# A fused attention and gated-recurrence kernel: ScalarE's zT copies put first, the head's loads in one queue, and six tiles of the output added by DMAs

## The reference

```python
x = x + layernorm(attention(layernorm(x)))
x = x + layernorm(gated(layernorm(x)))
```

```python
q = (x @ Wq.T).reshape(N, S, H, hd).transpose(0, 2, 1, 3)     # same for k, v
att = softmax(einsum('nqhd,nkhd->nhqk', q, k) / sqrt(hd), axis=3)
out = einsum('nhqk,nkhd->nqhd', att, v).reshape(N, S, D) @ Wo.T + bo
```

```python
ft = sigmoid(xt @ wf.T + c @ uf.T + bf); it = sigmoid(xt @ wi.T + c @ ui.T + bi)
gt = tanh(xt @ wc.T + c @ uc.T + bc);    c = ft * c + it * gt
h = tanh(einsum('tbi,oi->tbo', x, wo) + c_final @ uo.T + bo)
```

## Time and profile before

| what | us |
|---|---|
| median of 3 runs | 1361.56 |
| lowest and highest | 1359.27 and 1363.56 |
| the profiled execution, its own time | 1356.45 |
| its span, slowest core (core 6) | 1354.9 |
| spans of the 8 cores | 1345.2 to 1354.9 |
| mean granted TensorE clock of the cores | 0.989 to 0.993 |

### The profile page before, as it was taken

How to read it: one execution, slowest core, us unless ns; L and a number is a source line. 1 busy time by engine, 2 the same in 40 slices (tenths; PEclk the granted TensorE clock), 3 DMA queues, 4 the chain that set the end, 5 groups by cost and what they waited for, 6 DMA issues and landing times.

```text
span 1354.9 us, 25960 instructions; the slowest of 8 cores (1345.2 to 1354.9 us)
## 1 busy us (share of the span) xinstructions
PE 1296.4 (96%) x8256; PEld 733.4 (54%) x8256; DVE 834.1 (62%) x1460; ACT 571.9 (42%) x1572; POOL 400.9 (30%) x879
## 2 busy tenths in 40 slices
PE   4989999999899999899999999999999999999995
PEld 2577777776677777454444444444444444444442
DVE  5357778988799976574554545545455453226887
ACT  1246666665566665563222222222222222212665
POOL 3014444555455543331110101101011010001876
PEclk9999999999999999999999999999999999999998
DMA  9985676899789867728331222312222112009878
GB/s 198 197 143 115 147 152 143 190 188 184 187 196 197 203 195 266 265 71 277 128 125 47 94 91 80 125 48 94 92 80 94 48 63 78 0 15 346 272 253 248
DMA packets 126085, 200.96 MB, mean 148 GB/s; under 512 B 72672, under 2 KB 78816, under 8 KB 122848
## 3 DMA queue, kind: packets, MB, share of 16 engines
q1 hardware_dynamic: 109536, 172.56, 40.5%
q0 software_dynamic: 16416, 26.74, 14.6%
HBM read 157.34 MB, written 83.89 MB: 178 GB/s over the span
## 4 chain that ended last, share of the span: by engine, by line
PE 82%; DMA 5%; DVE 3%; SPq 3%; issue 2%; ACT 2%; POOL 2%; DVEq 0%; POOLq 0%; ACTq 0%
PE ps_big L445 11%; PE ps_s L445 11%; PE ps_s L433 11%; PE ps_big L433 11%; PE ps_big L320 11%; PE ps_big L346 7%; PE ps_big L308 6%; PE ps_big L329 3%; PE ps_s L504 3%; PE ps_big L504 2%; PE ps_o L504 2%; DMA exr<-xr 2%; PE ps_o L382 2%; SPq L1145 1%; PE ps_s L365 1%
## 5 line engine op out<-in xcount | busy, mean ns | idle before, releaser
L991 POOL TENSOR_SCALAR pn<-p,rl 128x128 bf16<-128x128 f32 x512 | 180.5, 368 | 298.2 <-DVE rl L601 297.6
L876 ACT ACTIVATE p<-ps_s,nm 128x128 f32<-128x128 f32 x512 | 181.0, 366 | 115.1 <-DVE nm L605 106.8
L346 PE MATMUL ps_big<-wo,zT 128*128 128x512 bf16 x512 | 122.9, 384 | 13.5 <-ACT zT L887 10.2
L691 DVE SCALAR_TENSOR_TENSOR ti<-ti,tg 128x512 f32<-128x512 f32 x64 | 44.2, 690 | 141.8 <-ACT tg L927 141.8
L308 PE MATMUL ps_big<-wv,xT 128*128 128x512 bf16 x512 | 123.1, 388 | 0.7 <-DVE zb L587 0.5
L320 PE MATMUL ps_big<-xT,wq 128*128 128x256 bf16 x1024 | 122.1, 274 | 0.0
L320 PE MATMUL ps_big<-xT,wk 128*128 128x256 bf16 x1024 | 121.2, 273 | 0.0
L605 DVE TENSOR_REDUCE nm<-ps_s 128x4 f32<-128x512 f32 x128 | 88.4, 691 | 29.0 <-PE ps_s L365 26.0
L876 ACT ACTIVATION_READ_ACCUMULATOR p<-ps_s,nm 128x1 f32 x512 | 104.2, 203 | 0.0
L320 PEld LDWEIGHTS ps_big<-xT,wq 128*128 128x128 bf16 x1024 | 98.2, 98 | 11.0
L320 PEld LDWEIGHTS ps_big<-xT,wk 128*128 128x128 bf16 x1024 | 97.7, 98 | 10.8
(11 more groups left out here) (162 smaller groups left out, 2479.1 us busy)
## 6 DMA issues: line engine op xcount, KB each, us to landing
z_scr<-zb SPq DMA_DIRECT2D x32, 512.0 KB, 6.2
h<-x_scr SPq DMA_DIRECT2D x29, 512.0 KB, 6.8
out<-h SPq DMA_DIRECT2D x28, 512.0 KB, 4.1
xin<-x SPq DMA_DIRECT2D x26, 512.0 KB, 6.6
zb<-z_scr SPq DMA_DIRECT2D x24, 512.0 KB, 4.2
xrb<-xr SPq DMA_DIRECT2D x24, 512.0 KB, 3.5
x_scr<-xrb SPq DMA_DIRECT2D x24, 512.0 KB, 2.9
vst<-v_scr SPq DMA_DIRECT2D x64, 128.0 KB, 6.6
```

What stands on the lines that cost most here:

```text
L346: mm = t.matmul(bank[:], zT[u % 2][:, ft * 128:(ft + 1) * 128], wo[:, ft * D + half * 512:ft * D + half * 512 + 512], start=ft == 0, stop= ...
L876: ex = a.activation(p32[G % 2][:, c], psS[G % 2][:, c], AF.Exp, bias=nm[G % 2][:, pk:pk + 1], accum_out=ls[G % 2][:, pk:pk + 1])
L991: op = g.tensor_scalar(pn[G % 2][:, c], p32[G % 2][:, c], rl[G % 2][:, pk:pk + 1], 1.0, AL.mult, AL.mult)
```

## The change

Four things change.

1. *The head's loads.* SP loads only tiles 0 and 1 of x, without a wait, and goes straight on to the masks. Tiles 2 to 7 are issued by POOL, behind V0; V1, K0, K1, Q0 and Q1 are issued one by one between the calls of rstd1, and wo last.
2. *The head's order.* DVE takes apply1(u) and stats1(u + 2) in turns. TensorE flips tiles 0 and 1 first, and tile i from 2 to 7 right ahead of group i. The copy of the flips 0 to 7 moves from DVE to ACT. In ACT's slots the copy of zT (oevict) now stands first, in all odd slots from 5 to 127; the even slots from 112 lose it, but for 128 and 130.
3. *Two buffers.* xl[4] and xl[5] move from the xln buffers to the region of exr. ACT's evict of F(., 1) no longer waits for flip2(5); in its place DVE's cell(0, 4) does, and SP waits for p_ap and d_ex1 instead of s_t1.
4. *The output.* ACC are now tiles 24 to 29 (before 24, 26, 27), VectorE's are 3, 7, 11, 15, 19, 23, 30, 31 (before ... 28, 29, 31). With it the residual of 25, 28 and 29 goes into the output directly, and their loads and stores fall away.

```diff
-H_DVE = (3, 7, 11, 15, 19, 23, 28, 29, 31)
-H_ACC = (24, 26, 27)
+H_DVE = (3, 7, 11, 15, 19, 23, 30, 31)
+H_ACC = (24, 25, 26, 27, 28, 29)
...
-          + [xln[0], xln[1], vtok[0], vtok[1]])
+          + [at(f"xl{i}", [128, D], BF16, oXR + o) for i, o in ((4, 6144), (5, 4096))]
+          + [vtok[0], vtok[1]])
...
-        for u in range(4):
-            flip1(u)
+        flip1(0)
+        flip1(1)
         for i, key in enumerate(head_groups()):
-            if 3 <= i < 7:
-                flip1(i + 1)
+            if 2 <= i < 8:
+                flip1(i)
             group(key)
...
-        for u in range(0, 8, 2):
-            for step in (stats1, apply1, flip1_out):
-                step(u)
-                step(u + 1)
+        stats1(0)
+        stats1(1)
+        for u in range(8):
+            apply1(u)
+            if u < 6:
+                stats1(u + 2)
...
-        h_res(28)
-        h_res(29)
         h_res(31)
+        h_res(30)
...
+        flip1_out(0)
+        flip1_out(1)
+        for i, key in enumerate(head_groups()):
+            if 2 <= i < 8:
+                flip1_out(i)
             evict(key)
         for G in range(NG + 3):
             n, s = G // 16, G % 16
             gs = slot_groups(G)
+            if 5 <= G < NG and G % 2 == 1:
+                oevict((G - 5) // 2)
             if len(gs) > 0:
                 evict(gs[0])
...
-            if 5 <= G < 112 and G % 2 == 1:
-                oevict((G - 5) // 2)
-            elif G >= 112 and G % 2 == 0:
+            if G >= NG and G % 2 == 0:
                 oevict((G - 4) // 2)
...
+        wload("V", 0)
         g.memset(mhalf[:], -0.5).then_inc(s_mh, 1)
+        for u in range(2, 8):
+            g.dma_start(out=xhead[u][:], in_=x_d[u]).then_inc(d_xh[u], 16)
...
-        for u in range(8):
-            rstd1(u)
+        rstd1(0)
+        rstd1(1)
+        for u, (kind, c) in enumerate((("V", 1), ("K", 0), ("K", 1), ("Q", 0), ("Q", 1))):
+            wload(kind, c)
+            rstd1(u + 2)
+        rstd1(7)
...
         h_acc(27)
+        h_acc(28)
         h_rstd(15, 30, 1)
         h_rstd(16, 31, 1)
-        h_out(30)
+        h_acc(29)
...
-        for u in range(8):
+        for u in range(2):
             xload_head(u)
```

More of the change, by code:

```diff
@@ L697, in cell @@
                 v.wait_ge(d_exl, 16 * 8)
+            elif i == 4:
+                v.wait_ge(p_t2, 6)
             v.wait_ge(s_S, i + 1)
@@ L847, in evict @@
                     a.wait_ge(p_t2, 4)
-                elif i == 1:
-                    a.wait_ge(p_t2, 6)
-                else:
+                elif i >= 2:
                     a.wait_ge(s_S, i - 1)
@@ L897, in scalar, with flip1_out @@
         a.activation(junk[:], mhalf[:, 0:1], AF.Exp)
-        for key in head_groups():
+        def flip1_out(u):
+            n, tt = u // 4, u % 4
+            a.wait_ge(s_t1, u + 1)
+            dst = xT[n % 2][:].rearrange("p (f t) -> p f t", f=8)[:, :, tt * 128:(tt + 1) * 128]
+            a.copy(dst, psT[:].rearrange("p (f t) -> p f t", f=8)).then_inc(s_t1e, 1)
+        flip1_out(0)
[3 more added lines that the diff above has]
+                flip1_out(i)
             evict(key)
@@ L965, in gpsimd, with wload @@
     def gpsimd(g):
[L966 to L972, removed]
+        def wload(kind, c):
+            dst, src = {"V": (wv, wv_d), "K": (wk, wk_d), "Q": (wq, wq_d)}[kind]
+            g.dma_start(out=dst[:].rearrange("p (f m) -> p f m", f=8)[:, :, c * 512:c * 512 + 512],
+                        in_=src.rearrange("(f p) m -> p f m", p=128)[:, :, c * 512:c * 512 + 512]
+                        ).then_inc(d_w[f"{kind}{c}"], 16)
+        wload("V", 0)
         g.memset(mhalf[:], -0.5).then_inc(s_mh, 1)
+        for u in range(2, 8):
+            g.dma_start(out=xhead[u][:], in_=x_d[u]).then_inc(d_xh[u], 16)
         g.wait_ge(s_mh, 1)
@@ L1016, in precast @@
                         ).then_inc(d_pre[w], 16)
-        for u in range(8):
-            rstd1(u)
+        rstd1(0)
[4 more added lines that the diff above has]
+        rstd1(7)
+        g.dma_start(out=wo[:].rearrange("p (f m) -> p f m", f=8),
+                    in_=wo_d.rearrange("(f p) m -> p f m", p=128)).then_inc(d_w["Z"], 16)
         for G in range(NG + 3):
@@ L1087, in xload_head @@
         def xload_head(u):
-            if u == 2:
-                s.wait_ge(d_xh[0], 16)
-            elif u == 4:
-                s.wait_ge(d_xh[2], 16)
-            elif u == 6:
-                s.wait_ge(d_w["V0"], 16)
             s.dma_start(out=xhead[u][:], in_=x_d[u]).then_inc(d_xh[u], 16)
@@ L1230, in sync @@
                     u_stage(0)
-                    s.wait_ge(s_t1, 32)
+                    s.wait_ge(p_ap, 8)
+                    s.wait_ge(d_ex1, 16 * 8)
                     s.wait_ge(d_vs[0], 16 * 12)
@@ L1310, in sync @@
         for half in range(2):
-            s.wait_ge(h_pd, 9 + half)
+            s.wait_ge(h_pd, 7 + half)
             s.dma_start(out=out_d[3, :, half * 512:half * 512 + 512],
                         in_=h1[7][:, half * 512:half * 512 + 512]).then_inc(d_ho[7], 16)
-        s.wait_ge(h_pp, H_DONE[30])
+        s.wait_ge(h_pd, 9)
         s.dma_start(out=out_d[2], in_=h1[6][:]).then_inc(d_ho[6], 16)
```

## The result

The changed kernel took 1369.08 us (median of 4 runs, 1368.23 to 1371.63) where the kernel before took 1360.41 beside it (4 runs, 1357.57 to 1363.56): the ratio is 1.0075, with a 95% interval of 1.0054 to 1.0095. (In some runs of most kernels here the cores of one die ran at a lower granted clock and the time was longer; the ratios and medians leave such runs out, except two of the 17 runs of the kernel before beside e5 to e8, three of e9's five, one of e11's six and one of e12's four.) It is slower by 8.7 us by the two medians and by about 10 by the ratio. 1363.3 us was forecast, with a range of 1356.0 to 1371.0; the time lies in the range, but "no change" was given nearly the same chance as "slower", and the sum of +1.7 us was 7 to 8 us short.

The account below looks back on a forecast made before the run. TensorE, busy 96% of the span, was taken as the bound, so only its idle or low-clock time could be won. Head +7.7, zT copies -4.8 and -1.7, F groups +1.7, tail -1.2 gave +1.7: 1363.3 us, range 1356.0 to 1371.0.

Parts of the forecast that it names:

- The tiles' landing and the head: Head: masks slow V0, tile 2 lands late and flip copies are exposed, so K groups start at 67.9; +7.7 us.
- Rival A: Head: masks' packets are through before V0's come in numbers, head 5.7 us earlier, 1357.6 us; chance 0.15.
- The copy on ScalarE: Head, six rounds: each flip's copy takes 1.06 us on ScalarE with nothing hiding it, 3.64 us a round.
- rival C: Head: the clock falls in the six rounds; three at half clock give 6.6 us more, 1369.9 us; chance 0.13.
- The zT copies: Attention: with the copies first, TensorE's zT waits go, -4.8 us up to 510 and -1.7 before 545.
- Rival D: Attention: copies first win nothing, TensorE waits for evict or exps instead; 4.8 us more, 1368.1 us; chance 0.10.
- The start of the F groups: Behind the attention: wait for wc grows to 6.2 us and a stretch at 1.2 GHz follows; +1.7 us (0 to 3.4).
- Rival B: F groups: wc lands in 11.8 us instead of 16.26, no new clock drop; 6.2 us less, 1357.1; chance 0.20.
- The tail: Kernel's end: new division of the adds ends the span 1.2 us earlier; -1.2 (-1.8 to +1.4).
- the last store is 1.8 earlier: Tail: single-column steps on GpSimd shrink by some 1.8 us, so the last h_apply and last store come 1.8 earlier.
- The sign that I named: Tail: the last landing would be that of an accumulating DMA, tile 29's, at 1352.6 us.
- The upper bound that I gave, +1.4: Tail: the cost in us if four accumulating DMAs in a row line up.

Follow-up runs that it names:

- e5: Kernel before with 4 of the 32 transfers that cast the recurrence's weights, part of the output left out: ratio 0.9949.
- e8: Changed kernel with each flip, and its copy on ScalarE, one group earlier: ratio 1.0001 to the kernel before.
- e9: Kernel before with the zT copies first and the 32 weight-casting transfers moved forward, 22 of them in slots 1 to 32: ratio 1.0160.
- e11: Changed kernel with flips one group earlier, masks issued after tile 7 of x, adding DMAs only for tiles 24 to 27: ratio 1.0024 to the kernel before.
- e12: e11 with the casting transfers moved forward as in e9: ratio 1.0145 to the kernel before.
- e1: Changed kernel with the old head (loads, order, flip copies on VectorE), the rest of the change kept: ratio 1.0015 to the kernel before.
- e7: Changed kernel with the three masks issued only when tile 7 of x has landed: ratio 1.0003 to the kernel before.
- e3: Kernel before with ScalarE's zT copies first, nothing else of the change: ratio 0.9989.
- e4: Kernel before with the change's division of the output adds (ACC 24 to 29; VectorE 30, 31), nothing else: ratio 1.0025.

## Why the prediction was right and wrong

*The tiles' landing and the head: right as a mechanism, 0.5 to 1.5 us short.* The forecast put the masks' slow stretch on V0: V0 at 20.7 (measured 21.2 to 23.5 over the cores, 23.4 on core 5), tile 2 at 22.8 (22.4 to 25.4), V groups at 26.5 (27.5 by the median), K groups at 67.9 (68.2). The term was +7.7 against the 60.19 of core 6; against the median core (59.0) it is +9.2, and e1 prices it at 8.2. Rival A (the masks are through before V0 comes) had V0 at 15.0: V0 did that only when e7 moved the masks away. The Trainium skill ("DMA: Bandwidth & Descriptors", section "Queues, rings and completion order") has a DMA engine go round between queues packet by packet. The trace agrees roughly, with 474 packets of the one queue and 373 of the other in 8.5:17, and an equal share of 99.7% for both.

*The copy on ScalarE: right.* It took 1.03 us (forecast 1.06; VectorE's 0.69). The six rounds were 3.62 each (forecast 3.64). The estimate by the Trainium skill ("Perfetto Trace Analysis", section "Optimizing Scalar/DVE Operations") was 0.98, so the row of SBUF data was a little nearer. Its advice to offload to ScalarE where VectorE is saturated was not tested by itself: no run has the new order with the copies on VectorE. By the two durations the engine is worth 0.34 us per copy, 2 us in six rounds, and e8 shows that the place costs more: with the flip one group earlier the slower copy costs nothing.

*The clock in the rounds: right not to count on it, rival C refuted.* TensorE idled 1.29 us in each round, and the granted clock of 30:54 on core 5 was

```profile
30.00:54.00 24.00, 16.76 (x102) 8.35 (x100) 12.09 (x23) 9.37 (x14) 7.89 (x14) 1.00 1.15 165
```

at 1.00.

*The zT copies: right for an undisturbed core, wrong for the slowest.* The forecast of -4.8 and -1.7 is what core 5 of e3 shows, 6.7, and the ten undisturbed cores with the copies first against the six with the copies last (median 382.9 and 389.7 us). The failed step is that I took the waits for zT in one core's trace for what the kernel's time would win. The time is that of the slowest of 8 cores; each core meets late loads at other places, and the traces have more of them with the copies first (11 to 17, against 8 to 10). That a TensorE that runs quicker leaves the loads less room is my reading of this; no run shows it. On the slowest core -1.5 is left. TensorE's wait of 3.0 us for kst stood in the trace of the kernel before, on the very core of the rows, and so did VectorE's 10.0 us for exr; I had not asked what they would do to a gain. Rival D had about the price (the copies first win nothing) but another mechanism: on core 5 of the changed kernel TensorE waited 0.2 us for an evict and 0.7 for exps of ScalarE, and its long waits go back to late loads.

*The start of the F groups: right in size.* +1.7 was forecast and +1.8 measured between slot 112 and the recurrence. But the wait is not one of 6.2 us for wc: it is 3.0 for wi, 1.7 for wc and 1.3 for ustc on core 5, 6.0 together, and wc took 14.1 us to land where the forecast kept 16.26. The clock fell again, to 0.73 and 0.93 in the two stretches of 5 us from 560, which costs 0.27 x 5 + 0.07 x 5 = 1.7 us as forecast. Rival B (wc comes along in 11.8, and the clock stays) did not happen.

*The tail: wrong, with the wrong sign.* -1.2 was forecast, and it costs 3.4 (e4). The step "the last store is 1.8 earlier" is right for its issue. What failed is what came after the issue: I left the store's landing at its old 3.0 us, while two adding DMAs (of tiles 28 and 29) were still under way beside it, where before none was, and it took 7.8. The price for the adding DMA was my median of 7.0; it was 9.3. The sign that I named, that an adding DMA would land last, did not come: the last store did, on every core. The upper bound that I gave, +1.4, was set for the adding DMAs in a row, not for the stores beside them. The -1.2 does not follow from its own terms either: a last landing at 1352.6, and the 0.6 us that the span of core 6 had behind its last landing, give -1.7.

*The sum.* 7.7 - 4.8 - 1.7 + 1.7 - 1.2 = +1.7 was forecast; the runs give 8.2 - 1.5 + 3.4 = +10.1, where the copies' -1.5 holds the F groups' part already. The tail is 4.6 us of the difference, the copies on the slowest core 3.3, the head 0.5. That 1369.08 still lies within the stated range is luck: it lies outside the forecast's own 1360.3 to 1366.5, and the range reached up there only for rivals C and D, whose mechanisms (the clock falls in the rounds; TensorE waits for evicts and exps) did not happen.

## What to carry to other kernels

Where a program ends with its slowest core, read a wait's worth on all cores: a gain on the chain of one core is taken only if the slowest core can use it, and waits that come irregularly (late loads beside large transfers) must be counted before the gain is priced. A transfer that adds in memory is no free addition at the end of a program; count what it does to the last stores beside it, not only when it is issued. When a queue is filled early, ask which transfer that was harmless late now stands beside the one that everything waits for.

## What the runs showed of the hardware that I had not expected

- Three mask loads of 128 KB in 8 rows of 16 KB beside a weight load left the core's DMA traffic at 91 GB/s over 8.5 us, and made the 1 MB load take 19.6 to 21.9 us instead of 13.1 to 14.7 (e7, masks issued later).
- The last plain store of 512 KB took 3.0 us at the end of the kernel before (2.9 to 3.7 over the cores), and 7.8 and 8.2 on the slowest cores of the change and of e4 beside adding DMAs of the software queue, the last of which took 9.3 and 9.7 there.
- With 22 casting transfers in 32 slots, the mean traffic between 110 and 170 us rose only from 133 to 143 GB/s, but the loads of v (128 KB) took 19.3 us instead of 6.3 (14.1 to 21.6 over the cores).
- For each us that VectorE stood idle in stretches of over 2.5 us, slots 16 to 112 took 1.06 us longer with the copies first and 0.73 us with the copies last.
- TensorE's clock stayed at 2.4 GHz (granted clock 1.00 from 30 to 60 us) through six idle stretches of 1.29 us, one every 3.6 us.
